# Moving x in transfers of 4 MB instead of 2 MB in a residual kernel with per-sample maps, on one Trainium2 core

## The reference, cut to what matters

```python
# x: (128, 128, 2048) f32; W0: (16, 128, 128); W1: (32, 128, 128); biases: (32, 1, 128)
def layer0(x, weights, condition):
    return jnp.einsum('bct,bcd->bdt', x, weights[condition])

def layer1(x, subjects, weights, biases):
    b = biases[subjects]
    return jnp.einsum('bct,bcd->bdt', x, weights[subjects]) + jnp.transpose(b, (0, 2, 1))

x = x + layer0(x, W0, itok_B_0_15)
x = x + layer1(x, itok_B_0_31, W1, biases)
```

## Time and profile before

| | us |
|---|---|
| median of 3 runs | 642.72 (642.55 to 642.77) |
| the profiled execution, its time | 642.87 |
| its span, first to last instruction | 641.1 |
| busy TensorE matmul / VectorE / ScalarE / GpSimd | 537.6 / 329.2 / 333.2 / 123.9 |

### The profile page before, as it was taken

One profiled execution on the slowest core, in us unless ns is written; L12 is line 12 of the kernel. 1 busy time (PEld: TensorE's weight loads), 2 busy tenths in 40 slices (PEclk: granted clock), 3 DMA queues, 4 the chain that ended last, 5 costly groups with the idle time before them and its releaser, 6 DMA issues.

```text
span 641.1 us, 6225 instructions
## 1 busy us (share of the span) xinstructions
PE 537.6 (84%) x2308; PEld 234.0 (37%) x2308; DVE 329.2 (51%) x259; ACT 333.2 (52%) x385; POOL 123.9 (19%) x263
## 2 busy tenths in 40 slices
PE   1899999999889888898898888988988988889870
PEld 0344444443334333343333333333433433334330
DVE  0366666665455445545554555455445544554460
ACT  0466666666455455554554555556545555555450
POOL 2222222222121121221221212212212112122000
PEclk9999999999999999999999999999999999999995
DMA  9999999999999999999999999999999999999995
GB/s 359 428 414 430 428 432 429 429 430 432 431 429 432 431 430 431 431 430 431 430 431 431 430 429 432 430 433 429 431 433 428 429 433 430 429 432 430 430 429 255
DMA packets 18931, 271.82 MB, mean 424 GB/s; under 512 B 2241, under 2 KB 2274, under 8 KB 2274
## 3 DMA queue, kind: packets, MB, share of 16 engines
q1 hardware_dynamic: 9504, 137.37, 50.4%
q10 hardware_dynamic: 9410, 134.26, 49.0%
HBM read 137.40 MB, written 134.22 MB: 424 GB/s over the span
## 4 chain that ended last, share of the span: by engine, by line
DMA 73%; PE 20%; DVE 3%; POOLq 0%; issue 0%; ACT 0%; DVEq 0%; POOL 0%; SPq 0%; ACTq 0%
DMA out_dram<-xt 42%; DMA xt<-in_x_dram 30%; PE acc L160 17%; PE acc L155 3%; DVE xt L224 2%; DMA w_sb<-in_w_dram 1%; DVE xt L226 1%; DVEq L39 0%; ACT L246 0%; POOLq L127 0%; POOLq L130 0%; POOL map0T L137 0%; POOL map L138 0%; ACT both L247 0%; ACT both L246 0%
## 5 line engine op out<-in xcount | busy, mean ns | idle before, releaser
L160 PE MATMUL acc<-xt,both 64*128 64x512 f32 x2048 | 471.7, 602 | 70.6 <-DMA xt<-in_x_dram 68.2
L251 ACT ACTIVATE xt<-acc,bias_of 64x1024 f32<-64x1024 f32 x256 | 283.6, 1108 | 272.3 <-PE acc L160 269.9
L224 DVE TENSOR_SCALAR xt<-acc,bias_of 64x1024 f32<-64x1024 f32 x128 | 163.3, 1276 | 279.8 <-PE acc L160 279.8
L160 PEld LDWEIGHTS acc<-xt,both 64*128 64x128 f32 x2048 | 189.5, 187 | 321.5 <-issue 224.1
L226 DVE TENSOR_SCALAR xt<-acc,bias_of 64x1024 f32<-64x1024 f32 x128 | 165.0, 1289 | 1.9
L137 POOL TENSOR_TENSOR map0T<-w0T_sb,ident 128x128 f32<-128x128 f32 x128 | 65.4, 511 | 467.8 <-PE acc L155 456.1
L155 PE MATMUL acc<-map,map0T 128*128 128x256 f32 x256 | 73.3, 409 | 0.9 <-POOL map L138 0.9
L138 POOL TENSOR_TENSOR map<-w_sb,ident 128x128 f32<-128x128 f32 x128 | 65.3, 510 | 0.0
L155 PEld LDWEIGHTS acc<-map,map0T 128*128 128x128 f32 x256 | 43.8, 191 | 52.3 <-issue 47.8
L247 ACT ACTIVATE both<-acc 64x256 f32<-64x256 f32 x64 | 24.2, 378 | 0.7
L246 ACT ACTIVATE both<-acc 64x256 f32<-64x256 f32 x64 | 24.1, 377 | 0.7
(11 more groups left out here) (4 smaller groups left out, 0.4 us busy)
## 6 DMA issues: line engine op xcount, KB each, us to landing
xt<-in_x_dram SPq DMA_DIRECT2D x64, 2048.0 KB, 27.0
out_dram<-xt ACTq DMA_DIRECT2D x64, 2048.0 KB, 40.5
w_sb<-in_w_dram SPq DMA_DIRECT2D x1, 2048.0 KB, 9.3
w0T_sb<-in_w0T_dram SPq DMA_DIRECT2D x1, 1024.0 KB, 4.8
cond_sb<-in_conds_dram ACTq DMA_DIRECT2D x1, 1.0 KB
bias_sb<-in_bias_dram ACTq DMA_DIRECT2D x1, 16.0 KB, 9.4
cond_rep<-in_conds_dram ACTq DMA_DIRECT2D x1, 16.0 KB, 11.1
```

The costliest lines, as they stand in the source:

```text
L160: return nc.tensor.matmul(acc[:, j * CHUNK:(j + 1) * CHUNK], both[k * HC:(k + 1) * HC, buf, u, :], xt[k * HC:(k + 1) * HC, slot, u * T + j ...
L224: nc.vector.tensor_scalar(xt[0:HC, q % SLOTS, a:a + HALF], acc0[0:HC, a:a + HALF], bias_of[0:HC, 2 * q:2 * q + 1], None, ALU.add)
L251: return nc.scalar.activation(xt[HC:C, q % SLOTS, v * T + a:v * T + a + HALF], acc1[v * HC:(v + 1) * HC, a:a + HALF], ACT.Identity, bias=b ...
```

## The change

x is loaded and stored four samples at a time. The slots of `xt` are used in four twos (`QUADS` = 4). A load is one DMA of 4 MB into two neighbouring slots: in SBUF 32 KB of each partition, in HBM two runs of 16 KB for each partition, 2 MB apart. `x_loaded` and `stored` have one semaphore for each two slots. TensorE waits for the load only ahead of the first pair of a four (even slot), and its work is otherwise unchanged. ScalarE issues one 4 MB store after the second pair of each four, and waits for `hi_out0` and `hi_out1` only there. The last four samples are stored as before, as two DMAs of 2 MB, on semaphores of their own. There are 32 loads instead of 64, and 33 stores instead of 64.

```diff
+    QUADS = SLOTS // 2
-    x_pairs = x.rearrange("(q k) (i u) t -> q (k i) (u t)", k=2, u=2)
+    x_quads = x.rearrange("(g q k) (i u) t -> g (k i) q (u t)", q=2, k=2, u=2)
+    out_quads = out.rearrange("(g q k) (i u) t -> g (k i) q (u t)", q=2, k=2, u=2)
     out_pairs = out.rearrange("(q k) (i u) t -> q (k i) (u t)", k=2, u=2)
...
-        x_loaded = [sem(f"x_loaded{q}") for q in range(SLOTS)]
-        stored = [sem(f"stored{q}") for q in range(SLOTS)]
+        x_loaded = [sem(f"x_loaded{g}") for g in range(QUADS)]
+        stored = [sem(f"stored{g}") for g in range(QUADS)]
+        last_stored = [sem(f"last_stored{k}") for k in range(2)]
...
-            for q in range(PAIRS):
-                slot = q % SLOTS
-                if q >= SLOTS:
-                    sp.wait_ge(stored[slot], LOAD * (q // SLOTS))
-                sp.dma_start(xt[:, slot, :], x_pairs[q, :, :]).then_inc(x_loaded[slot], LOAD)
+            for g in range(PAIRS // 2):
+                quad = g % QUADS
+                if g >= QUADS:
+                    sp.wait_ge(stored[quad], LOAD * (g // QUADS))
+                sp.dma_start(xt[:, 2 * quad:2 * quad + 2, :], x_quads[g, :, :, :]).then_inc(x_loaded[quad], LOAD)
...
-                pe.wait_ge(x_loaded[slot], (turn + 1) * LOAD)
+                if slot % 2 == 0:
+                    pe.wait_ge(x_loaded[slot // 2], (turn + 1) * LOAD)
...
-                act.wait_ge(hi_out0, q + 1)
-                act.wait_ge(hi_out1, q + 1)
-                act.dma_start(out_pairs[q, :, :], xt[:, q % SLOTS, :]).then_inc(stored[q % SLOTS], LOAD)
-            for q in range(SLOTS):
-                act.wait_ge(stored[q], LOAD * TURNS)
+                last = q >= PAIRS - 2
+                if q % 2 == 1 or last:
+                    act.wait_ge(hi_out0, q + 1)
+                    act.wait_ge(hi_out1, q + 1)
+                if last:
+                    act.dma_start(out_pairs[q, :, :], xt[:, q % SLOTS, :]).then_inc(last_stored[q % 2], LOAD)
+                elif q % 2 == 1:
+                    quad = q % SLOTS // 2
+                    act.dma_start(out_quads[q // 2, :, :, :],
+                                  xt[:, 2 * quad:2 * quad + 2, :]).then_inc(stored[quad], LOAD)
+            for g in range(QUADS - 1):
+                act.wait_ge(stored[g], LOAD * TURNS)
+            act.wait_ge(stored[QUADS - 1], LOAD * (TURNS - 1))
+            for k in range(2):
+                act.wait_ge(last_stored[k], LOAD)
```

## The result

The changed kernel takes 644.05 us in the median of 18 runs (642.7 to 644.7), the kernel before, run beside it, 642.74 us (642.37 to 642.97). The ratio is 1.0017, with a 95% interval of 1.0011 to 1.0023 (it isn't the quotient of the two medians). By the ratio the change costs 1.1 us, by the medians 1.3 us: clear of the noise, and within or just at the edge of the 0.2% that I had called the same. The profiled execution took 644.62 us, with a span of 642.8 us.

The account below looks back on a forecast made before the run. The prediction took DMA at 431 GB/s as the bound and summed -0.5 (fewer DMAs), +0.3 (start) and +0.5 (end) to +0.3 us, forecasting a median of 643.0 us, with an 8-in-10 range of 639.0 to 646.8.

Parts of the forecast that it names:

- What bounds it: Whole kernel: DMA sets the pace at 431 GB/s, while TensorE would need 8.13 us of a pair's 9.83.
- Fewer DMAs: Throughout: 63 fewer DMAs, with 63 fewer small packets on each engine, save 0.5 us, out of 0 to 0.9.
- The start: Near 60 us: the store queue may lack its second store when the first ends; +0.3 us, out of 0 to 2.3.
- The end: Ahead of the last store: the store queue may run dry before it begins; +0.5 us, out of 0 to 3.5.
- The clock: Middle: TensorE's waits of 3.3 us are too short for its clock to fall, and slower matmuls would fit; no cost.
- The dry ring: Near 60 us or ahead of the last store: a late store start idles the engines; +2 to +4 us, chance 0.25.
- the packets kept their rate: Rival, throughout: runs 2 MB apart in HBM slow the packets to 416 GB/s, 665 us; chance 0.05.
- the trailing engine's lag: Rival, at the end: one engine's 4.6 us lag shrinks with fewer DMAs, giving back 2 to 4.6 us; chance 0.18.
- the signs that I had named for being wrong: Middle rate not 431 GB/s, a changed lag of the trailing engine, or over a us without packets at start or end.

Follow-up runs that it names:

- e12: The changed kernel with each product of maps made during the second pair of a four issued three times instead of once; 646.82 us, ratio 1.0063.
- e1: The changed kernel with the first eight samples stored as four DMAs of 2 MB, each once its pair is done; 642.98 us, ratio 0.9998.
- e2: The changed kernel with only the load of the last four samples issued as two DMAs of 2 MB; 643.70 us, ratio 1.0011.
- e3: The changed kernel with first and last loads each split into two DMAs and the first eight samples stored as four; 642.60 us, ratio 0.9995.
- e4: The changed kernel with the last four samples stored as one DMA of 4 MB; 646.24 us, ratio 1.0046.
- e9: The changed kernel with 18 extra identity matmuls on TensorE before the first pair, every DMA as it is; 642.83 us, ratio 1.0009.
- e10: The changed kernel with the extra matmuls of e9 and 16 more behind the first product of maps; 644.55 us, ratio 1.0024.
- e7: The changed kernel with loads and stores of eight samples in two slots of 8 MB, the last eight samples stored as four DMAs; 742.38 us, ratio 1.1541.

## Why the prediction came out as it did

*What bounds it.* Right: 431 GB/s from 80 to 600 us in both kernels, whatever TensorE did beside it (e12).

*Fewer DMAs, -0.5 us.* The size is too large, and even the sign is barely shown. From 80 to 600 us seven kernels with 4 MB both ways in the middle (the changed one, e1, e2, e3, e4, e9, e12) moved 224.05 to 224.16 MB, the kernel before 224.01: 0.04 to 0.15 MB, 0.1 to 0.35 us for 53 small packets fewer on each engine. e10, at 223.97, is below the kernel before, so that this is within what one profile can tell. The fit that the prediction set beside this term, from the Trainium skill ("DMA: Bandwidth & Descriptors", Anatomy of one DMA), is one for DMAs issued by GpSimd. Those of x are issued by SyncE and ScalarE, and no run here has DMAs in series to compare.

*The start, +0.3 us, out of 0 to 2.3.* This is the step that was mis-sized, and it carries the result: 1.6 us in the profile. The mechanism and the place stood in the text, the second store having to be at hand when the first ends near 60 us. I had the second store issued 1.8 us ahead and chose a start after 1.2 us. The start time was about right (the store issued at 59.12 moves from 60.0 us on, e4's last one after 0.8 us), but the margin was not: the issue time hangs on how long the first matmuls take, 5.36 us for sixteen before and 6.77 in the changed kernel's profile. I took the 5.36 of the earlier trace rows as fixed. The 1 us that I gave a landing came from no row either: here the first store's last packets start before 59.75 us and it lands at 60.8. The 5.36 left me 0.6 us of margin; 1.3 us of delay used it up and left the idle moment of 0.7 us. The rest of the loss was in no term of mine: the 1.1 us lost from 64 to 67 us, when the next load joins at a low rate. e10 and e12 show such stretches too after their idle moments (344 and 180 GB/s from 65 to 67 us in e10), e2 and e9, which have no idle moment, don't; why, the runs don't tell. The table shows the loss by 80 us grow with the lateness of the second store: none at 56.5, 0.2 us at 57.7, 1.4 at 58.9, 1.6 at 59.1, 2.0 at 59.9, 3.9 at 61.9.

*The end, +0.5 us, out of 0 to 3.5.* The gap was there, 2 us long at a share of 0.16, but it cost next to nothing in the span: I had reckoned with the queue of an average engine, and the span ends with the one that trails. e2 removed the gap, and its span is its start's. e9 has a gap of 1 us and a span of 640.3, 0.8 us shorter than the kernel before:

```profile
631.00:632.00 1.00, 0.00 (x0) 0.00 (x0) 0.21 (x1) 0.00 (x0) 0.00 (x0) 1.00 0.09 33
```

With the larger dose of e4 the end does count, 1.9 us instead of my 5.

*The clock.* I said that waits of 3.3 us are too short for it to fall. Wrong: the mean granted clock from 64 to 624 us is 0.95 instead of 1.00. In a stretch of one such wait of the changed kernel the matmuls end near 297.4 and the next sixteen begin at 300.57 us:

```profile
298.00:300.00 2.00, 0.00 (x0) 0.00 (x0) 1.99 (x2) 1.70 (x2) 0.00 (x0) 0.98 1.07 459
300.00:302.00 2.00, 1.43 (x4) 0.85 (x6) 0.02 (x1) 0.00 (x0) 0.00 (x0) 0.50 0.95 410
```

It is at the lower level, 1.2 GHz, before the load lands. The sixteen take 6.75 us there, and 3.70 in a pair at a granted clock of 1.00:

```profile
300.57 6.75 PE L164 MATMUL acc<-xt,both 64*128 64x512 f32 x16 [3.16 <-DMA xt<-in_x_dram]
```

The part that mattered in the middle held: the slower matmuls are hidden there. For the first pair of the kernel the column of the granted clock reads 1.00 in both profiles, at 5.36 and at 6.77 us. That these matmuls ran at the lower level is thus inferred: from their length, which is that of the sixteen above, and from e9 and e10, where matmuls issued ahead of them brought the same sixteen to 3.70. The Trainium skill ("TensorE: Matmul & The Clock Gate", HAM oscillation — how this bites in real kernels) describes just this, waits for DMA between stretches of compute that throttle the clock again; the trace agrees, and shows that it is free where DMA is the bound.

*The rivals.* The dry ring (0.25) is what happened in the profiled execution, at about half of its price; the packets kept their rate in the middle; and the trailing engine's lag did change. In stretches of half a microsecond the other engines are done near 635.0 us in the kernel before and near 638.5 in the changed one, and the last stores land at 640.6 and 642.3: a lag of 5.6 us (my 4.6 was read from wider stretches) and of 3.8. The first line is of the kernel before:

```profile
635.00:635.50 0.50, 0.00 (x0) 0.00 (x0) 0.00 (x0) 0.00 (x0) 0.00 (x0) 0.50 0.08 33
638.50:639.00 0.50, 0.00 (x0) 0.00 (x0) 0.00 (x0) 0.00 (x0) 0.00 (x0) 0.50 0.08 33
```

The lag shrank because the others stood still in the gap, not because the trailing engine ended earlier, and so nothing was won. By the signs that I had named for being wrong, two came true: the lag changed, and at the end most engines were without packets for more than a microsecond. That the forecast still lay 1 us from the median is in part luck: the start was put too low by 1.3 us, the end too high by 0.5, and the saving of fewer DMAs too high by 0.15 to 0.4.

What stays open is the spread. The kernel before spans 0.6 us over its 18 runs beside the changed kernel, which spans 2.0 us. Differences in the length of the first matmuls, carried on by the late second store, would do that, but e9, which takes them away, has no narrower spread (641.91 to 645.63), and e1's profile shows that an execution can lose 2 us in its first 34 for another reason. Long executions aren't tied to the change: of the 29 runs of the kernel before beside e1 to e4, six took more than 644 us, up to 644.93; none of them was profiled, so that the reason may be another. The profile of the changed kernel has no such early loss, with 0.23 MB more by 58 us than before.

## What to carry to other kernels

Where DMA is saturated in the middle, as here, look at the ends to choose the size of its transfers. Doubling the transfer in this ring of fixed size changed nothing while both queues held work (a second doubling, e7, left them without it), but it put off the first store from 32.27 to 42.87 us and halved the number of pieces that bridge the moment when the loads have filled the ring. Work out by what margin the next transfer is issued before the last one ends, and what varies in that margin, rather than whether there is one; with small transfers at the start and at the end (e3) the large ones between cost nothing, and won nothing.

## What the runs showed of the hardware

- TensorE's granted clock fell from 1.00 to 0.50 within a wait of 3.16 us (from 297.4 to 300.57 us). The first sixteen matmuls of x took 5.19 to 6.77 us in kernels that do the same up to there, with the granted clock shown as 1.00, and 3.70 us with 18 matmuls of the identity ahead of them.
- Two loads of 64 partitions in place of one of 128 cost 12% of the whole time, with load packets 20% longer on average. While only loads ran, they moved 209 GB/s in place of 431.
- One DMA of 16 rows of 64 bytes behind each load cost 0.11 us each in the middle, and moved the backlog from the store queue to the load queue (a load took 53.2 us to land in place of 27.0, a store 14.0 in place of 40.5).
- The removed closing packets of a DMA were worth at most 7 ns each on an engine (0.35 us for 53), and in e10 nothing.
- A store issued when its queue was empty or nearly so moved its first packets 0.8 to 0.9 us later (632.72 to 633.5 in e4, 59.12 to 60.0 in the changed kernel).
- When a load joined a store stream some 4 us after an idle moment, the two together ran at 229 to 295 GB/s for about 3 us in the changed kernel.
